# Macaron transformer layer on one core: how the zero rows, the maxima's parts and the first four heads' operands are made

## The reference

```python
x = x + 0.5 * ffn(layernorm(x))          # ternary weights, 128 -> 512 -> 128, relu
x = x + attention(layernorm(x))          # 16 heads of 8, rope on q and k, softmax over 512 keys
x = x + 0.5 * ffn(layernorm(x))
```

## Time and profile before

| | |
|---|---|
| median of 3 runs | 543.53 us (539.21 to 546.67) |
| profiled execution | 541.95 us, its span 540.2 us |
| mean granted TensorE clock | 0.965 |
| busy: PE, DVE, ACT, POOL | 92%, 73%, 62%, 40% |
| first score (L539) starts | 46.88 us |
| first exponential starts | 60.95 us |

### The profile page before, as it was taken

How to read it: one execution, slowest core, us unless ns; L and a number is a source line. 1 busy time by engine, 2 the same in 40 slices (tenths; PEclk the granted TensorE clock), 3 DMA queues, 4 the chain that set the end, 5 groups by cost and what they waited for, 6 DMA issues and landing times.

```text
span 540.2 us, 8600 instructions
## 1 busy us (share of the span) xinstructions
PE 498.2 (92%) x3187; PEld 235.9 (44%) x3187; DVE 393.5 (73%) x579; ACT 334.9 (62%) x425; POOL 217.6 (40%) x292
## 2 busy tenths in 40 slices
PE   6686899989999989998999979999999999999986
PEld 3454434343453535352454533354435433443445
DVE  5672886957887678875787758877977898698124
ACT  2411346748857676765857655868686768577751
POOL 3403358434565183805552183418431831103202
PEclk7996889999999999998999998999999999999999
DMA  7859317402460139003360039013801480000000
GB/s 217 213 195 204 69 32 224 100 2 77 151 129 2 33 107 233 5 2 112 125 137 1 23 118 232 5 31 112 224 12 40 150 186 3 21 2 3 1 21 21
DMA packets 20681, 48.27 MB, mean 89 GB/s; under 512 B 2528, under 2 KB 5088, under 8 KB 19616
## 3 DMA queue, kind: packets, MB, share of 16 engines
q1 hardware_dynamic: 19328, 45.89, 32.0%
q10 hardware_dynamic: 1312, 1.84, 1.1%
HBM read 20.58 MB, written 18.87 MB: 73 GB/s over the span
## 4 chain that ended last, share of the span: by engine, by line
PE 62%; POOL 9%; DMA 8%; issue 7%; DVE 7%; ACT 5%; SPq 1%; POOLq 0%; ACTq 0%; DVEq 0%
PE heads_acc L575 17%; PE unit L558 11%; PE unit L539 11%; PE side L637 7%; DMA q_stack<-q_scratch 3%; DVE maxima L863 3%; PE side L631 3%; ACT probs L778 3%; PE side L617 2%; PE side L625 2%; PE side L613 2%; POOL normed_ffn L376 2%; DMA q_scratch<-q_parts 2%; DMA k_swap<-k 1%; PE heads_acc L645 1%
## 5 line engine op out<-in xcount | busy, mean ns | idle before, releaser
L863 DVE TENSOR_REDUCE maxima<-unit 128x2 f32<-128x1024 f32 x256 | 305.5, 1220 | 97.1 <-PE unit L539 96.1
L778 ACT ACTIVATE probs<-unit 128x1024 f32<-128x1024 f32 x256 | 256.6, 1027 | 112.1 <-PE unit L558 111.3
L575 PE MATMUL heads_acc<-probs,v_heads 128*32 128x512 f32 x1024 | 136.6, 611 | 1.3 <-ACT probs L778 1.1
L558 PE MATMUL unit<-q_stack,k_stack 64*128 64x512 f32 x512 | 119.9, 467 | 9.9 <-DMA q_stack<-max_T 5.7
L539 PE MATMUL unit<-k_stack,q_stack 62*128 62x512 f32 x512 | 115.3, 448 | 8.6 <-DMA q_stack<-q_scratch 5.7
L558 PEld LDWEIGHTS unit<-q_stack,k_stack 64*128 64x128 f32 x512 | 48.7, 187 | 79.4 <-issue 31.7
L539 PEld LDWEIGHTS unit<-k_stack,q_stack 62*128 62x128 f32 x512 | 49.7, 190 | 56.8 <-ACT probs L778 26.4
L1033 POOL TENSOR_SCALAR max_parts<-maxima 128x16 fp32r<-128x16 f32 x31 | 6.3, 205 | 129.5 <-DVE maxima L863 129.2
L637 PE MATMUL side<-w_q,hidden 128*128 128x128 f32 x416 | 57.2, 289 | 0.0
L637 PEld LDWEIGHTS side<-w_q,hidden 128*128 128x128 f32 x416 | 50.6, 197 | 13.6 <-issue 11.3
L575 PEld LDWEIGHTS heads_acc<-probs,v_heads 128*32 128x32 f32 x1024 | 21.0, 108 | 44.3 <-issue 36.1
(11 more groups left out here) (143 smaller groups left out, 443.5 us busy)
## 6 DMA issues: line engine op xcount, KB each, us to landing
k_scratch<-k_parts SPq DMA_DIRECT2D x16, 512.0 KB, 3.0
q_scratch<-q_parts SPq DMA_DIRECT2D x14, 512.0 KB, 2.8
k_stack<-k_scratch SPq DMA_DIRECT2D x14, 512.0 KB, 7.0
q_stack<-q_scratch SPq DMA_DIRECT2D x14, 512.0 KB, 9.4
resid<-in_x SPq DMA_DIRECT2D x8, 256.0 KB, 5.1
k_stack<-zero_rows SPq DMA_DIRECT2D x4, 480.0 KB
q_stack<-zero_rows SPq DMA_DIRECT2D x4, 480.0 KB
k_swap<-k SPq DMA_DIRECT2D x14, 128.0 KB, 2.3
```

Source lines behind the costliest of these rows:

```text
L558: mm = pe.matmul(to[:, e, :], k_stack[part, quad // NQ % 2, pair, kt * P:(kt + 1) * P], q_stack[part, quad // NQ % 2, pair, :], start=True ...
L575: mm = pe.matmul(heads_acc[32 * j:32 * j + 32, :], v_heads[:, b % 2, at, ODD * odd:ODD * odd + 32], probs[:, burst % RING, j, :], start=(k ...
L778: act.activation(probs[:, burst % RING, 2 * pp:2 * pp + 2, :], unit_of(PLACE["exp", n]), ACT.Exp, scale=SCALE).then_inc(s_exp, 1)
L863: dve.tensor_reduce(maxima[:, quad % 2, :, r], unit_of(PLACE["max", k]), AX_X, ALU.max).then_inc(s_max, 1)
```

## The change

1. The zero rows: `zero_rows` and its 8 DMAs are gone. GpSimd sets each slot of each stack to zero as a whole, all 128 partitions (`zeros`, four memsets of 128 x 4096), before the rows are loaded. The memsets of `v_heads` move behind the first norm's `ln_rstd`. The loads of x for batches 3 to 7 move ahead of SyncE's first wait.
2. `split_max` and `split_first_max` move from GpSimd to VectorE, right behind the quad's last reduction (the first quad's after the 4th and the 8th).
3. `max_row` of the next batch's first quad stands ahead of both swaps.
4. The first quad's operands of q and k: `first_part_to_scratch` writes only the rows of heads that the first quad reads (4 DMAs of 64 KB for k on SP's queue, 4 for q on ACT's), into the scratch's other half. The whole parts, 4 DMAs of 512 KB, follow on SP's queue, and the rest of the stacks after them.
5. The three tables are new, and there are more fills: 10 before the first score (4 before), 14 before the first `e` (8), and 4 each in steps 0, 2 and 3 of the first batch.

```diff
@@ SyncE
+            for j in range(3, B):
+                load_x(j)
+            sp.wait_ge(s_row_values, 1)
+            sp.wait_ge(s_zeros["k"], 2)
...
-            sp.wait_ge(s_rows_fill, ROWS_FILLED[0])
             for c, ready in enumerate((s_first_hi["k"], s_first_lo["k"])):
                 sp.wait_ge(ready, 1)
-                part_to_scratch(sp, "k", 0, c)
-            sp.wait_ge(s_scratch["k"], 16 * PARTS)
+                first_part_to_scratch(sp, "k", c)
+            sp.wait_ge(s_first_scratch["k"], 16 * 2 * PARTS)
             for e in range(2):
-                rows_to_stack(sp, "k", 0, e, slice(0, 2), s_stack_first)
+                rows_to_stack(sp, "k", 0, e, slice(0, 2), s_stack_first, 1)
+            sp.wait_ge(s_first_hi["q"], 1)
+            sp.wait_ge(s_first_lo["q"], 1)
+            for n in "kq":
+                for c in range(PARTS):
+                    part_to_scratch(sp, n, 0, c)
+            sp.wait_ge(s_stack_first, STACK_LANDED)
+            sp.wait_ge(s_zeros["q"], 2)
             stack(0, slice(2, NPAIR), s_stack[0])
-            zero_between(1)
...
-                if on("proj", b):
-                    swap("k", b + 2)
                 if on("values", b):
                     max_row((b + 1) * NQ)
                 if on("proj", b):
+                    swap("k", b + 2)
                     swap("q", b + 2)
@@ new: four of these DMAs for k, four for q
+        def first_part_to_scratch(engine, n, c):
+            for h in range(2):
+                to = scratch[n][1, c, :, h::NPAIR, :] if n == "q" else scratch[n][1, :, c, h::NPAIR, :]
+                part = qk_parts[n][h::NPAIR, c, :].bitcast(F32).unsqueeze(1).to_broadcast([P // NPAIR, PARTS, S])
+                engine.dma_start(to.rearrange("c p t -> p c t"), part).then_inc(s_first_scratch[n], 16)
@@ VectorE, in max_of
                 dve.tensor_reduce(maxima[:, quad % 2, :, r], unit_of(PLACE["max", k]), AX_X, ALU.max).then_inc(s_max, 1)
+                if quad == 0 and r % T == T - 1:
+                    split_first_max(r // T)
+                elif quad > 0 and r == QSTEPS - 1:
+                    split_max(quad)
@@ GpSimd, ahead of its loop
+            zeros("k", 0)
+            pool.wait_ge(s_minus_half, 1)
+            ln_rstd("ffn1", 0)
             pool.memset(v_heads[:], 0.0).then_inc(s_v_fill, 1)
...
-            pool.wait_ge(s_minus_half, 1)
-            ln_rstd("ffn1", 0)
             ln_rstd("ffn1", 1)
             pool.wait_ge(s_b2h, 1)
             add_bias("ffn1", 0)
+            zeros("k", 1)
             ln_rstd("ffn1", 2)
             ln_rstd("attn", 0)
             add_bias("ffn1", 1)
+            zeros("q", 0)
+            zeros("q", 1)
             ln_rstd("attn", 1)
@@ the first line of the table STEADY
-    "e m ffn1_T", "e m pv heads_copy1@-1 ffn1_up0", "e m", "e heads_T1@-1 pv m", "e m ffn1_up1 pv max_T1 ffn1_stats@5",
+    "e m ffn1_T", "e m", "e pv m heads_copy1@-1 ffn1_up0", "e m pv max_T1", "e m", "e heads_T1@-1 pv m", "e m pv",
```

More of the change, by code:

```diff
@@ L236, in macaron_layer @@
         s_rows_fill = sem("stack_rows_filled")
+        s_zeros = {n: sem(f"{n}_stack_slots_set_to_zero") for n in "qk"}
         s_v_fill = sem("v_heads_filled_with_constants")
@@ L406, in part_to_scratch, with rows_to_stack @@
             engine.dma_start(to.rearrange("c p t -> p c t"), part).then_inc(s_scratch[n], 16)
-        def rows_to_stack(engine, n, j, e, hs, landed):
+        def first_part_to_scratch(engine, n, c):
[3 more added lines that the diff above has]
+                engine.dma_start(to.rearrange("c p t -> p c t"), part).then_inc(s_first_scratch[n], 16)
+        def rows_to_stack(engine, n, j, e, hs, landed, half=None):
             tile = q_stack if n == "q" else k_stack
-            products = scratch[n][j % 2].rearrange("q k (d e h) t -> (q k d) e (h t)", d=DH, e=2)
+            products = scratch[n][j % 2 if half is None else half].rearrange("q k (d e h) t -> (q k d) e (h t)", d=DH, e=2)
             engine.dma_start(tile[64 * e:64 * e + PROD, j % 2, hs, :].bitcast(F32).rearrange("p h t -> p (h t)"),
@@ L417, in load_x @@
                 sp.dma_start(batch_rows(j), x[j].rearrange("(p t) d -> p t d", t=T)).then_inc(s_x[j], 16)
-            def zero_between(slot):
-                for tile in (k_stack, q_stack):
-                    for e in range(2):
-                        to = tile[TILE_ROWS * e + PROD:TILE_ROWS * e + ROWS_MAX, slot, :, :].bitcast(F32)
-                        sp.dma_start(to, zero_rows[:].unsqueeze(1).to_broadcast([ROWS_MAX - PROD, NPAIR, S])).then_inc(s_rows_fill, 16)
             load_x(0)
@@ L443, in _ @@
                 sp.dma_start(to, minus_rows[:].unsqueeze(1).to_broadcast([PARTS, 2 * NPAIR, S])).then_inc(s_rows_fill, 16)
-            zero_between(0)
-            for j in range(3, B):
-                load_x(j)
             def swap(n, j):
@@ L852, in ln_stats, with split_first_max, split_max @@
                     dve.bn_aggr(mean_var[n][:, t, :], stats[n][:, t, :]).then_inc(s_var[n], 1)
+            def split_first_max(p):
+                dve.wait_ge(s_max, (p + 1) * T)
+                whole = maxima[:, 0, :, p * T:(p + 1) * T]
+                dve.tensor_scalar(first_parts[:, p, :, 0, :], whole, 1.0, 0.0, ALU.mult, ALU.add).then_inc(s_first_split, 1)
+                dve.wait_ge(s_first_split, p * SPLIT_STEPS + 1)
+                dve.tensor_tensor(first_parts[:, p, :, 1, :], whole, first_parts[:, p, :, 0, :].bitcast(F32),
+                                  ALU.subtract).then_inc(s_first_split, 1)
+            def split_max(quad):
+                dve.wait_ge(s_max, (quad + 1) * QSTEPS)
+                wait(dve, s_maxT_psum, quad - 1)
+                whole = maxima[:, quad % 2, :, :]
+                dve.tensor_scalar(max_parts[:, :, 0, :], whole, 1.0, 0.0, ALU.mult, ALU.add).then_inc(s_split, 1)
+                dve.wait_ge(s_split, (quad - 1) * SPLIT_STEPS + 1)
+                dve.tensor_tensor(max_parts[:, :, 1, :], whole, max_parts[:, :, 0, :].bitcast(F32),
+                                  ALU.subtract).then_inc(s_split, 1)
             def max_of(k):
@@ L1027, in add_bias, with zeros @@
                 pool.tensor_tensor(xb[n][:], batch_rows(j), bias.to_broadcast([P, T, D]), ALU.add).then_inc(s_xb[n], 1)
-            def split_max(quad):
-                pool.wait_ge(s_max, (quad + 1) * QSTEPS)
-                wait(pool, s_maxT_psum, quad - 1)
-                whole = maxima[:, quad % 2, :, :]
-                pool.tensor_scalar(max_parts[:, :, 0, :], whole, 1.0, 0.0, ALU.mult, ALU.add).then_inc(s_split, 1)
-                pool.wait_ge(s_split, (quad - 1) * SPLIT_STEPS + 1)
-                pool.tensor_tensor(max_parts[:, :, 1, :], whole, max_parts[:, :, 0, :].bitcast(F32),
-                                   ALU.subtract).then_inc(s_split, 1)
-            def split_first_max(p):
-                pool.wait_ge(s_max, (p + 1) * T)
-                whole = maxima[:, 0, :, p * T:(p + 1) * T]
-                pool.tensor_scalar(first_parts[:, p, :, 0, :], whole, 1.0, 0.0, ALU.mult, ALU.add).then_inc(s_first_split, 1)
-                pool.wait_ge(s_first_split, p * SPLIT_STEPS + 1)
-                pool.tensor_tensor(first_parts[:, p, :, 1, :], whole, first_parts[:, p, :, 0, :].bitcast(F32),
-                                   ALU.subtract).then_inc(s_first_split, 1)
+            def zeros(n, slot):
+                tile = q_stack if n == "q" else k_stack
+                pool.memset(tile[:, slot, :, :].bitcast(F32), 0.0).then_inc(s_zeros[n], 1)
+            zeros("k", 0)
+            pool.wait_ge(s_minus_half, 1)
+            ln_rstd("ffn1", 0)
             pool.memset(v_heads[:], 0.0).then_inc(s_v_fill, 1)
```

42 lines of the change are left out of this document (17 added, 25 removed), and 32 rows, old and new, of tables (FIRST, LATER, STEADY).

## The result

The changed kernel takes 561.1 us (median of 4 runs, 559.23 to 561.99) against 541.9 us for the kernel before in the same session (539.21 to 546.67). The ratio is 1.034, with a 95% interval of 1.026 to 1.042: slower. The prediction said 531 us, 519 to 544.

What follows compares the result with a forecast made beforehand. The prediction took the kernel to be bound by PE's own work, leaving only idle time, half clock and the start to win. Its terms summed to -10.7 us: 540.2 - 10.7 + 1.75 = 531 us, range 519 to 544.

Steps and rivals of the forecast that it cites:

- The zero rows: Three places ahead of the first score: GpSimd's memsets hold VectorE's norms for their whole length, +7.8 us, bounds 0 and 11.3.
- the memsets hold nobody back: Rival at the start: memsets do not hold up VectorE, all else as forecast, 523 us; chance 0.30.
- The first quad's operands: Ahead of the first score: small pieces sent alone land sooner, first score at 43.1, -3.8 us (-4.0 to -1.6).
- The opening: First score to first exponential: fills and the earlier stack close PE's gap, ending half clock, -2.3 us, between 0 and 2.7.
- The first exponential steps: First batch's 20.8 us stretch at clock 0.75: full clock returns, VectorE is the floor, -2.3 us.
- the fills: Steps 0, 2 and 3 of the first batch: added fills take 1.6 us, 0.6 fits in PE's idle time, +1.0 us.
- Two waits in the first batch: PE's waits for the next stack (0.89 us) and at `max_T3` (1.27 us): second gone, first partly, -1.5 us.
- Row loads ahead of swaps: First transposed scores of batches: rows go out 3.4 us earlier, so PE's waits in four batches go, -5.6 us.
- the later clock: Batches from 251.9 and 313.8: clock dips and stalls go with the row and split waits, -1.6 and -3.9 us.
- The swaps lose nothing: SyncE's queue: the row loads' issues take 1.39 us and are over before k is ready, so swaps are not delayed.
- Splits on VectorE: Each of 32 quads: VectorE's idle time covers the splits, waits behind GpSimd seldom coincide, +1.5 us, bounds 0 and 10.
- The rival that ends slower: Every quad: VectorE's splits stand behind two GpSimd instructions and stall PE, 17 us on top of 531, 548 us; chance 0.08.

Runs made afterwards that it cites:

- experiment 3: The changed kernel with the three tables of before and no fills in the steps: 556.4 us; with memsets also moved clear of VectorE's norms: 538.7 us.
- experiment 7: The changed kernel with memsets moved clear of the norms, the old tables, and the stack in two halves around the third quad's row load: 535.4 us, 0.989.
- experiment 9: The kernel before with only the row load of the next batch's first quad moved ahead of both swaps: 547.8 us, 1.012.
- clear_memsets: The changed kernel with three of the stacks' four memsets and those of `v_heads` waiting until that moment's norm is done: 549.0 us, 1.018.
- clear_halves: The changed kernel with memsets moved clear of the norms and the next batch's stack in two halves, the third quad's row load between: 531.2 us, 0.979.
- rows_on_act: The changed kernel with each batch's third-quad row load, from batch 1 on, issued by ScalarE behind its copy of `max_T`: 563.0 us, 1.041.

## Why the prediction was wrong

The direction was wrong. Step by step downwards from the changed kernel: 561.1 - 12.1 (memsets) - 17.8 (rows and stack) = 531.2 us. Without its memset term my sum was 531 - 7.8 = 523. Of the 8 us between, 6.4 could be the splits, by what they cost alone in the kernel before (7.9 instead of 1.5, about half of it with a row behind it). It is an account and no proof: experiments 3, 7 and 9 show that the parts don't simply add.

- *The zero rows, +7.8.* The mechanism was right, the size was not. By the timeline the first place cost 2.1 us, the second 1.1, the third 6.7: together 9.9, less 0.5 because the first norm began that much earlier, and 1.8 more because PE, having waited 6.37 us, made the transposes and projections behind at half clock (1.08 instead of 0.63 us for four transposes). q's last part was ready at 45.34 instead of 34.18, +11.2; in the time it was 12.1. The step that failed is "its second would fit behind that norm": in the trace's single instructions the first two of the norm's four, begun at 26.4 and 27.6, end only when the second memset does, at 34.5. The engine that waits did not get its turn between two memsets that follow each other without a gap. The rival "the memsets hold nobody back" is refuted. My bounds, 0 and 11.3, held the 11.2; they had the second memset's 3.5 in them.
- *The first quad's operands, -3.8.* From q's last part to the first score it was 9.55 us instead of 12.70: -3.15, inside the bounds. The small pieces land quickly, but four issues take ScalarE 2.70 us where two took 1.10, and the stack's rows still meet SyncE's 2 MB:

```profile
44.65 2.70 ACTq L414 DMA_DIRECT2D q_scratch<-q_parts  x4
```

- *The opening, -2.3.* Right: 11.8 us from first score to first exponential at clock 1.00, against 14.1.
- *The first exponential steps, -2.3, and the fills, +1.0.* Right in sum: the clock came (1.00 instead of 0.75), and the ninth exponential starts 18.5 us after the first instead of 20.2, 1.7 us off against 1.3 forecast. VectorE was the bound there, as I had said, busy for 18.80 of 20.8 us.
- *Two waits in the first batch, -1.5.* This did not come. The wait at `max_T3` (1.27 us) went, but PE waits 1.14 us for the next batch's stack instead of 0.89, and 0.98 us for ScalarE's `hidden` where it did not wait before. Batch 0 as a whole gained 1.3 us, of the 2.8 that this item and the last add up to.
- *Row loads ahead of swaps, -5.6, and the later clock, -1.6 and -3.9.* This is the step that turned the sign. At the batch's start the waits went, as predicted. I then took the saved time as time off the batch, and did not ask which date comes next. That date is the third quad's row load, which lands about when the next batch's stack, issued ahead of it, has landed. In batches 1 to 4 PE comes to it 24 to 26 us into the batch, where the stack lands at 27.4 to 27.7 (25.8 to 28.0 before). So the saved 1.6 us became waits of 1.1 to 3.6 us, and the clock dips I expected to lose came back at them, at more places. In the kernel before the schedule stood just behind this floor: in batches 1 and 2 the rows landed 27.3 and 26.9 us into the batch, and the 17th transposed score came at 27.8. Experiment 9 shows it with nothing else changed. With the halves batches 1 to 6 take 336.6 us against 342.3 in the kernel before: 5.7 of the 11.1 that these terms promised, with the splits' cost in it.
- *The floor was in my rows.* Only three of the four waits of the earlier trace rows stand at a batch's start. The fourth, of 0.8 us, is the third quad's in batch 5: its rows went out at 19.1 us into the batch and landed at 24.3, behind the stack's last piece at 23.9. I wrote that it goes because `max_T` stands a step earlier; the issue was not what it waited for.
- *In batches 5 and 6 the change also makes the stack later*, which I had no term for: its last piece lands 27.1 and 27.9 us into the batch, against 23.9 and 23.4 before. The new LATER has `max_T1` a step later, and in SyncE's order the row load behind it stands ahead of q's scratch DMAs. In batch 5, which begins at 370.1 before and at 382.5 after:

```profile
375.22 1.41 SPq L472 DMA_DIRECT2D q_stack<-max_T  x2
377.10 1.68 SPq L406 DMA_DIRECT2D q_scratch<-q_parts  x2
...
391.48 1.41 SPq L473 DMA_DIRECT2D q_stack<-max_T  x2
392.99 0.87 SPq L407 DMA_DIRECT2D q_scratch<-q_parts  x2
```

  After the change GpSimd had q's first part ready at 390.0, and it went out 3.0 us later; before, it went out at once. No run takes this part from the rest.
- *"The swaps lose nothing".* True with the new LATER, where `max_T4` stands ahead of `k`; false with the old one (experiment 9). I had looked at a STEADY boundary alone.
- *Splits on VectorE, +1.5.* The mechanism, VectorE's instruction held for GpSimd's whole one, was in the text; the mistake was to call both waits together rare. GpSimd's rotation is a run of instructions with next to no gaps, just when a batch's first split comes. And VectorE's share of the quad (3.4 us idle) was the wrong measure: what counts is that the next reduction stands behind 2.4 us. The term measured 8 us alone in the kernel before, inside the stated bounds of 0 to 10; half of it no row explains.
- *The rival that ends slower* put 548 us on the splits at 0.08, by a cost of 17 us on top of 531. They cost some 8, half of that; the other losses came on top. That the kernel ended slower is no merit of this rival. No rival had a transfer's landing as the next floor, though that is what cost the most.

## What to carry to other kernels

Before counting a removed wait as gain, list what the waiting engine needs next and when each of these lands by its own clock; a wait that goes is worth only the distance to the next date. Big transfers are dates of their own: where a small urgent one falls due in the midst of a large one, put it between two halves of the large one, and give each half its own semaphore. And place GpSimd's memsets where VectorE idles or reads PSUM, not beside a run of its SBUF instructions.

## What the runs showed of the hardware

- A GpSimd memset, which reads nothing, held VectorE's tensor_scalar on SBUF for its whole length: 3.51 us for 128 x 4096, 6.96 for two in a row. A VectorE copy on SBUF took 2.74 us instead of 0.40 in `clear_memsets`, where the memset of `k_stack` ran beside it. A VectorE instruction that had begun to wait at 26.37 was passed by memsets that began at 27.50 and 30.95. The Trainium skill (SBUF — State Buffer, "Who interferes with whom") has it that whoever issues first gets the ports; here, by the profile's start times, the one that waited longer did not, and the measurement decides.
- VectorE's fp32 tensor_tensor on two SBUF operands was held by GpSimd's tensor_tensor too: 1.20 us beside it, 0.17 alone. The same section of the Trainium skill says so of two SBUF inputs against a GpSimd instruction that reads, and the trace agrees. Moving the split to VectorE therefore exposes both of its instructions. Beside a memset a tensor_tensor was not held: 0.69 us for 128 x 512 at 29.47 in `clear_memsets`, while `v_heads`' memset ran from 28.65 to 31.31, as long as the one at 32.13, with GpSimd idle.
- VectorE's reductions out of PSUM were not held: 1.21 us at 354.68 in `clear_halves`, while GpSimd ran an add of 1.29, and 1.22 on the mean.
- A DMA of 8 KB issued on ScalarE's queue landed 5 to 9 us later while SyncE's four pieces of 512 KB were under way (`rows_on_act`, batches 1 to 5). Another queue gave it no way past bytes that were already with the DMA engines.
